# Local attention of a fused transformer kernel: from one head at a time to head pairs

## The chip, the cores and the metric

The kernel runs on one core of a Trainium2 chip. A core has five engines with an instruction stream each: TensorE (PE in the profile; its weight loads are listed as PEld), VectorE (DVE), ScalarE (ACT), GpSimd (POOL) and SyncE (SP), which issues the DMAs. They meet only through semaphores. The metric is the device time of one execution in microseconds (us); lower is better. The median of three runs is 1999.87 us.

## The reference, cut to what matters

The program is four layers of attention and feed-forward on a tensor `x` of 8 batches x 256 tokens x 128 channels. The change touches one function that runs twice: the windowed ("local") attention inside the third layer's feed-forward block.

```python
DIM, DEPTH, HEADS, DIM_HEAD, WINDOW = 128, 2, 8, 64, 64
qkv = shift_token(x) @ wqkv                       # q, k, v: 8 heads of 64
q, k = l2norm(q) * qs, l2norm(k) * ksc
q, k = rotary_xpos(q, k)                          # t*cos*scale + rotate_half(t)*sin*scale
# every window of 64 queries sees its own 64 keys and the 64 before them
sim = einsum('bhwid,bhwjd->bhwij', q * 8, k)
mask = (i < j) | (i > j + WINDOW) | (j == -1)
attn = softmax(where(mask, -max, sim))
o = einsum('bhwij,bhwjd->bhwid', attn, v)
x = x + o @ wo
```

Tokens 0 to 127 of a batch need keys 0 to 127. Tokens 128 to 255 need keys 64 to 255, since a query reaches at most 64 keys back.

## The kernel before, in words

`local_attention` is called for `layer` 0 and 1, with other stages between. It has a prologue, then eight batches (a loop of three rounds of two batches, then two batches written out), then a tail. Everything is float32; a float32 matmul is two passes in the trace, so "x2" is one matmul, except that the turns (transpositions) are one pass each.

**One head.** Per batch and head, TensorE computes scores for the two tiles of 128 queries (L2396: 128x128 for the first, L2397: 128x256 for the second). The queries `q` lie in 128 rows per head, 64 of them zero, so that a whole-array matmul against the keys of a head pair picks one head. VectorE adds the band mask, negates, and takes the minimum in one instruction per tile (`maxima`, L2188). ScalarE takes the exponentials and their row sums (`exponentials`, L2285). TensorE turns the 128x384 probabilities in three pieces (L2419) into a bank of PSUM, VectorE copies them out (L2204), and once both heads of a pair are copied, TensorE multiplies by V (L2388, L2391) in the two column halves of its array. These V products are called `GROUP`, `GROUP+1`, `GROUP+2`, and `LAST` for the fourth pair, which is done in the next batch.

**The ring.** All other results of TensorE go through a ring of four PSUM banks, `ring`. A `fill` on TensorE waits until the bank has been drained four fills earlier (`ring.free`), and a `drain` on ScalarE or VectorE waits until it is full. A batch has 18 fills: `QK`..`QK+3` (projections of q and k two batches ahead, L2345), `TURN`..`TURN+3` (turns of the normalised q and k of the next batch, four turns each, L2351), `V`, `V+1` (L2357), `LAST`, `SUMS` (turns the inverse sums, L2362), `SPREAD`, `SPREAD+1` (L2370), `OUT` (output projection, L2377) and the three `GROUP` fills. ScalarE drains all of these but `SPREAD` and `OUT`, which are VectorE's. The table `after` says behind which head each fill stands; `order` and `due` come from it.

**Order on each engine, per head n:** TensorE: scores of head n+2, turns of head n, then the fills due at n. ScalarE: exponentials of head n+2, then the drains due at n. VectorE: maxima of head n+2, the copy of head n, then drains, or a share of the preparation of later batches: `sum_squares`, `own_part` and `normalise`, each once for each 128-token tile j. `normalise(b, j)` ends with a multiply (L2149) that TensorE's `TURN` fills wait for. GpSimd computes the rotated halves (L2034), an inverse square root by `pow` (L2085) and the split of the inverse sums into three bfloat16 parts (L2064 to L2070).

**Prologue and tail.** Before the first scores, batches 0 and 1 are prepared (`AHEAD_OF_LOOP`, and on VectorE the loop `for b in range(2)`). After the last batch, `LAST`, `SUMS`, both `SPREAD` and `OUT` of the last batch are done one after another.

Of the kernel before, what the change touches and what calls it, by code (L numbers as in the profile page):

```python
# [1952 lines left out]
def local_attention(m, layer):  # L1953
# [24 lines left out]
    after = {QK: 1, QK + 1: 1, QK + 2: 2, QK + 3: 2, LAST: 1, SUMS: 2, TURN: 1, TURN + 1: 3, TURN + 2: 3, TURN + 3: 4, SPREAD: 5,  # L1978
             SPREAD + 1: 5, V: 4, V + 1: 6, OUT: 6}
    after.update({GROUP + g: 2 * g + 3 for g in range(NG - 1)})  # L1980

    SQUARED, SUMMED, OWN = (1, 4), (2, 6), (4, 6)
    order = sorted(range(PER), key=lambda f: (after[f], f < GROUP, f))
    due = [[f for f in order if after[f] == n] for n in range(NH)]
# [4 lines left out]
    with ExitStack() as ctx:  # L1989
# [47 lines left out]
        with nc.Block() as block:  # L2037
# [64 lines left out]
            def _(dve):  # L2102
# [859 lines left out]
```

## Time and profile before

| what | us |
|---|---|
| median of 3 runs | 1999.87 (1999.37 to 2002.19) |
| the profiled execution | 2002.39 |
| its span, first to last instruction | 2000.6 |
| local attention, layer 0: first to last batch's turns | 1147.80 to 1313.75 of the span |
| local attention, layer 1 | 1414.65 to 1582.77 of the span |

The two stages together take a sixth of the span. The page's busy shares over the whole program (PE 84%, DVE 65%, ACT 54%, POOL 27%) say little on them; the rows further down are from within the stages. In those rows a matmul's duration runs to its last result in PSUM, while the next one may start as soon as its columns have streamed. So what a matmul costs the engine is read from start to start.

### The profile page before, as it was taken

How to read it: one execution, taken by the hardware profiler on the slowest of the kernel's cores; microseconds unless marked ns; L12 is line 12 of the kernel's file. 1: busy time of each engine (PE TensorE's matmuls, PEld its weight loads, DVE VectorE, ACT ScalarE, POOL GpSimd, SP SyncE). 2: the span in 40 equal slices, each digit the busy share in tenths (PEclk: the TensorE clock that was granted, in tenths of full speed). 3: DMA queues.
4: the chain of work that ended last, by engine and by line, in shares of the span. 5: the costliest groups of instructions: out<-in, count | busy, mean ns of one | idle time of the engine just before them, and what ended most of it. 6: DMA issues, size and time to landing. Idle time of an engine off the chain costs nothing. (4 is left out here: it accounts for less than half of the span.)

```text
span 2000.6 us, 32933 instructions
## 1 busy us (share of the span) xinstructions
PE 1677.7 (84%) x10815; PEld 902.4 (45%) x10865; DVE 1305.7 (65%) x3417; ACT 1082.2 (54%) x2292; POOL 533.2 (27%) x609
## 2 busy tenths in 40 slices
PE   6769999963799999999997599976899786999933
PEld 4423333321455555555554366643566532333311
DVE  5447666645656666665666698854799546777746
ACT  3404666658455565555553477743777442666723
POOL 0326545110100000000000667413766133233000
PEclk9777999986899999999999799998999985999965
DMA  4224333010100000000000000000000022222000
GB/s 146 41 65 102 66 72 69 14 55 0 33 6 1 6 6 1 7 6 1 1 1 1 23 1 0 0 12 22 1 0 0 19 41 63 44 50 44 11 11 21
DMA packets 60188, 53.29 MB, mean 27 GB/s; under 512 B 9818, under 2 KB 52750, under 8 KB 59926
## 3 DMA queue, kind: packets, MB, share of 16 engines
q1 hardware_dynamic: 59190, 51.17, 11.1%
q8 instruction: 77, 1.26, 0.3%
q10 hardware_dynamic: 864, 0.39, 0.1%
q14 instruction: 57, 0.47, 0.1%
HBM read 30.44 MB, written 1.05 MB: 16 GB/s over the span
## 5 line engine op out<-in xcount | busy, mean ns | idle before, releaser
L1469 DVE CUSTOM_DVE_ANT_0 minus_s_l2x<-s_ps_l2x,mask_b_l2x 128x512 f32<-128x512 f32 x256 | 166.7, 689 | 193.9 <-PE s_ps_l2x L1639 193.8
L1552 ACT ACTIVATE probs_l2x<-minus_s_l2x,nmax_l2x 128x512 f32<-128x512 f32 x256 | 182.7, 715 | 184.2 <-DVE nmax_l2x L1469 184.2
L1026 DVE CUSTOM_DVE_ANT_0 junk_l1x<-s_ps_l1x,mask_b_l1x 128x512 f32<-128x512 f32 x256 | 166.4, 688 | 78.7 <-PE s_ps_l1x L1212 77.1
L1029 DVE TENSOR_REDUCE nmax_l3x<-s_ps_l3x 128x1 f32<-128x512 f32 x256 | 163.5, 685 | 56.1 <-PE s_ps_l3x L1212 54.4
L1078 ACT ACTIVATE pT_l1x<-st_ps_l1x 128x1024 f32<-128x1024 f32 x128 | 131.1, 1024 | 72.9 <-PE st_ps_l1x L1198 72.3
L1512 DVE COPY pT_l2x<-t_ps_l2x 128x512 f32<-128x512 f32 x256 | 164.3, 683 | 1.0 <-PE t_ps_l2x L1648 1.0
L2285 ACT ACTIVATE probs_l2a<-minus_s_l2a,nmax_l2a 128x128 f32<-128x128 f32 (+1 forms) x256 | 113.9, 447 | 89.1 <-DVE nmax_l2a L2188 87.1
L1648 PEld LDWEIGHTS t_ps_l2x<-consts,probs_l2x 128*128 128x128 f32 x1024 | 109.6, 141 | 96.9 <-issue 88.3
L1078 ACT ACTIVATE pT_l3x<-st_ps_l3x 128x1024 f32<-128x1024 f32 x128 | 130.1, 1022 | 35.3 <-PE st_ps_l3x L1198 33.8
L1648 PE MATMUL t_ps_l2x<-consts,probs_l2x 128*128 128x128 f32 x1024 | 139.8, 279 | 0.2 <-ACT probs_l2x L1552 0.2
L2034 POOL TENSOR_TENSOR other_l2a<-qk_l2a,tb_l2a 128x256 f32<-128x256 f32 x120 | 100.2, 866 | 44.9 <-ACT qk_l2a L2244 42.4
L2085 POOL TENSOR_TENSOR rn_l2a<-ssc_l2a,consts 128x16 f32<-128x16 f32 x32 | 95.1, 2977 | 51.6 <-DVE ssc_l2a L2125 51.3
L2188 DVE CUSTOM_DVE_ANT_0 minus_s_l2a<-s_ps_l2a,consts 128x128 f32<-128x128 f32 (+1 forms) x256 | 80.6, 352 | 33.1 <-PE s_ps_l2a L2397 30.6
L1224 PE MATMUL pv_ps_l3x<-pT_l3x,v_l3x 128*32 128x256 f32 x1024 | 82.5, 396 | 2.7 <-ACT o_l3x L1086 2.2
L1418 POOL TENSOR_TENSOR x_tok<-x_tok,bo_l2x 128x256 f32<-128x256 f32 x8 | 5.8, 724 | 289.4 <-DVE xn_l2x L1455 289.4
L1224 PE MATMUL pv_ps_l1x<-pT_l1x,v_l1x 128*32 128x256 f32 x1024 | 81.2, 391 | 1.0 <-ACT o_l1x L1086 0.9
L2397 PE MATMUL s_ps_l2a<-kT_l2a,q_l2a 128*128 128x256 f32 x256 | 78.7, 390 | 0.0
L1212 PE MATMUL s_ps_l3x<-kT_l3x_first,q_l3x 51*128 51x512 bf16 x192 | 65.0, 432 | 13.3 <-DVE nmax_l3x L1029 8.4
L1639 PE MATMUL s_ps_l2x<-kT_l2x_first,q_l2x 64*128 64x512 f32 x256 | 73.2, 649 | 1.9 <-ACT q_l2x L1534 1.5
L1639 PE MATMUL s_ps_l2x<-kT_l2x,q_l2x 64*128 64x512 f32 x256 | 72.3, 641 | 2.0 <-DVE nmax_l2x L1469 1.8
L1190 PE MATMUL st_ps_l1x<-maskT_b_l1x,consts_bf 128*128 128x512 bf16 x215 | 68.1, 383 | 4.7 <-issue 3.1
L2204 DVE COPY pT_l2a<-t_ps_l2a 128x384 f32<-128x384 f32 x128 | 70.7, 552 | 0.0
(480 smaller groups left out, 3654.3 us busy)
## 6 DMA issues: line engine op xcount, KB each, us to landing
kT_l1x_first<-parts_l1x_first SPq DMA_DIRECT2D x72, 64.0 KB
kT_l3x_first<-parts_l3x_first SPq DMA_DIRECT2D x72, 64.0 KB
mask_i_l1x<-in_mask SPq DMA_DIRECT2D x8, 512.0 KB, 3.8
maskT_i_l1x<-in_mask_t SPq DMA_DIRECT2D x8, 512.0 KB, 4.8
q_l1x<-parts_l1x_first SPq DMA_DIRECT2D x90, 32.0 KB
q_l3x<-parts_l3x_first SPq DMA_DIRECT2D x90, 32.0 KB
ctxT_l0x<-in_ctxT SPq DMA_DIRECT2D x9, 256.0 KB, 3.0
rows_l0x<-in_ctx SPq DMA_DIRECT2D x9, 256.0 KB, 4.0
```

The lines of the kernel that those rows point to most:

```text
L1026: dve.tensor_tensor_reduce(out=junk[w][:], in0=s_ps[w][:], in1=mask_b[b % 2][:, j, :], scale=-1.0, scalar=3e38, op0=ALU.add, op1=ALU.min, ...
L1029: dve.tensor_reduce(to, s_ps[w][:], AX.X, ALU.max, negate=True).then_inc(m.s_drained[w].sem, 1)
L1078: act.activation(pT[t % 4][:, :, 2 * j:2 * j + 2, :].rearrange("p w c t -> p w (c t)"), st_ps[j][:], ACT.Exp)\
L1224: ins = pe.matmul(pv_ps[32 * hh:32 * hh + 32, 0:S], v[b % NV][:, c, (4 * g + hh) * 32:(4 * g + hh + 1) * 32], pT[(2 * group + hh // 2) % 4 ...
L1469: dve.tensor_tensor_reduce(out=minus_s[n % 4][:], in0=s_ps[n % 2][:], in1=mask_b[b % 2][:], scale=-1.0, scalar=3e38, op0=ALU.add, op1=ALU. ...
L1512: dve.tensor_copy(pT[g % 2][:, hh, :, j * P:(j + 1) * P], t_ps[c % 2][:].rearrange("p (c t) -> p c t", t=P))\
L1552: act.activation(probs[n % 4][:], minus_s[n % 4][:], ACT.Exp, bias=nmax[:, b % 2, n:n + 1], scale=-1.0, accum_out=sums[:, b % 2, j, h:h + ...
L1639: pe.matmul(s_ps[n % 2][:], q[b % 2][rows, g, j * P:(j + 1) * P], kT[b % 2][rows, g, :], start=True, stop=True)\
L1648: ins = pe.transpose(t_ps[n % 2][:, c * P:(c + 1) * P], probs[n % 4][:, c * P:(c + 1) * P], k["ident"])
L2034: eng.tensor_tensor(other[:, j, w, :, to], qk[:, j, w, :, of], tb[:, w, j, to].unsqueeze(1).to_broadcast([P, NH, 32]), ALU.mult).then_inc( ...
L2085: pool.tensor_tensor(rn[:, cols], ssc[:, cols], k["minus_half"][:, 0:2 * NH], ALU.pow).then_inc(m.powers_ready.sem, 1)
L2285: act.activation(probs[n % (2 * DEEP)][:, cols], minus_s[n % (2 * DEEP)][:, cols], ACT.Exp, bias=nmax[:, u, TPB * n + j:TPB * n + j + 1], ...
```

## The change

1. **Scores of a pair.** `q` is stored like `k`, two heads in the 128 rows and no zeros. The two heads' scores are separate matmuls in the upper and lower 64 rows of the array, one PSUM bank each.
2. **192 keys.** The second tile's scores, mask, exponentials cover keys 64 to 255 rather than 0 to 255. The columns of `probs` that are no longer written are zeroed once by GpSimd.
3. **Steps of a pair.** The loop goes over four steps rather than eight heads. TensorE: scores of pair s+1, the V product of the pair before (first fill of the step), turns of both heads of pair s, the other fills of `due[s]`. ScalarE: copy of the second head's turned probabilities, exponentials of pair s+1, drains. VectorE: maxima of pair s+1, copy of the first head's turned probabilities, its other work.
4. **Fill order.** `due` is written out: (`LAST`, `QK`, `QK+1`, `QK+2`), (`GROUP`, `TURN`..`TURN+3`, `SUMS`), (`GROUP+1`, `SPREAD`, `SPREAD+1`, `QK+3`, `V`), (`GROUP+2`, `V+1`, `OUT`). `SUMS` stands last in step 1.
5. **Preparation.** `normalise(b+2, 0)` is done in step 2 of batch b and `normalise(b+1, 1)` in step 0; before, both were of batch b+1, behind heads 0 and 1. The prologue therefore normalises tile 0 of batch 1 too, ahead of the first maxima. The reciprocal of the sums stands at the head of step 0, and GpSimd takes the `pow` of tile 0 before it rotates tile 1.
6. **ScalarE** drains q with one 128-row instruction in place of two of 64 rows.

```diff
-    TILES = (slice(0, P), slice(P, BAND))
+    TILES = (slice(0, P), slice(P + 64, BAND))
...
+    STEPS = NH // 2
+    due = [[LAST, QK, QK + 1, QK + 2],
+           [GROUP, TURN, TURN + 1, TURN + 2, TURN + 3, SUMS],
+           [GROUP + 1, SPREAD, SPREAD + 1, QK + 3, V],
+           [GROUP + 2, V + 1, OUT]]
...
                     for j in range(TPB):
                         sum_squares(b, j)
                         own_part(b, j, at)
-                    if b == 0:
-                        for j in range(TPB):
+                        if b == 0:
                             other_half(dve, j, 1)
+                        if (b, j) != (1, 1):
                             normalise(b, j)
...
+                        if s == 0 and left >= 1:
+                            normalise(b + 1, 1)
+                        if s == 2:
+                            for f in range(SPREAD, OUT):
+                                drain(i, u, f, turn(i, u, f))
+                            if left >= 2:
+                                normalise(b + 2, 0)
+                        if s == 3:
+                            if left >= 2:
+                                sum_squares(b + 2, 1)
+                                own_part(b + 2, 1, at)
+                            drain(i, u, OUT, turn(i, u, OUT))
...
+                    for s in range(STEPS):
+                        act.wait_ge(*ring.full(*group_before(i, u, s)))
+                        act.wait_ge(*m.turned.after(NH * b + 2 * s + 2))
+                        act.activation(pT[s % 2][:, 1].rearrange("p c t -> p (c t)"), t_ps[1][:, 0:BAND], ACT.Copy).then_inc(m.unit_copied[1].sem, 1)
+                        if s + 1 < STEPS or left >= 1:
+                            exponentials(*ahead(i, u, s + 1))
+                        for f in due[s]:
+                            drain(i, u, f, turn(i, u, f), unused=f < (LAST, TURN, 0)[left])
...
+                    halves = [(s_ps[hh], slice(HD * hh, HD * (hh + 1))) for hh in range(2)]
+                    for out, rows in halves:
+                        pe.matmul(out[:, 0:P], q[u][rows, g, 0:P], kT[u][rows, g, 0:P], start=True, stop=True)
+                    for out, rows in halves:
+                        pe.matmul(out[:, TILES[1]], q[u][rows, g, P:S], kT[u][rows, g, 64:S], start=True, stop=True).then_inc(m.scores_ready.sem, 1)
...
+                        if s + 1 < STEPS or left >= 1:
+                            pe.wait_ge(*m.max_ready.after(TPB * (NH * b + 2 * s + 2)))
+                            scores(*ahead(i, u, s + 1))
+                        fill(i, u, due[s][0], turn(i, u, due[s][0]), unused=due[s][0] < (LAST, TURN, 0)[left])
+                        pe.wait_ge(*m.probs_ready.after(TPB * (NH * b + 2 * s + 2)))
+                        for n in (2 * s, 2 * s + 1):
+                            pe.wait_ge(*m.unit_copied[n % 2].after(STEPS * b + s))
+                            for c in range(3):
+                                ins = pe.transpose(t_ps[n % 2][:, c * P:(c + 1) * P], probs[n % (2 * DEEP)][:, c * P:(c + 1) * P], k["ident"])
+                            ins.then_inc(m.turned.sem, 1)
+                        for f in due[s][1:]:
+                            fill(i, u, f, turn(i, u, f), unused=f < (LAST, TURN, 0)[left])
```

How the instructions stand; rows that only prepare registers or repeat the row above them are left out. First TensorE, before, from the second turns of batch 0 (`ring0` to `ring3` are the ring's banks, `t_ps` the banks of turned probabilities; `bankN_drained` is the ring's wait):

```order
L2419 MATMUL t_ps1_l2a0<-consts,probs1_l2a0 128x128 [waits turned_copied]
L2345 MATMUL ring0_l2a0<-wqkv_l2a0,hs0_l2a0 128x512 [waits bank0_drained]
L2345 MATMUL ring1_l2a0<-wqkv_l2a0,hs0_l2a0 128x512 [waits bank1_drained]
L2351 MATMUL ring2_l2a0<-consts,own_l2a0 128x128 [waits bank2_drained]
L2388 MATMUL ring3_l2a0<-pT1_l2a0,v1_l2a0 64x256 [waits bank3_drained]
L2396 MATMUL s_ps0_l2a0<-kT0_l2a0,q0_l2a0 128x128 [waits max_ready]
L2397 MATMUL s_ps0_l2a0<-kT0_l2a0,q0_l2a0 128x256
L2419 MATMUL t_ps0_l2a0<-consts,probs2_l2a0 128x128 [waits turned_copied]
```

And TensorE in the changed kernel, step 1 of batch 0, from its V product (`GROUP`, bank 0) to `SUMS` (bank 1):

```order
L2390 MATMUL ring0_l2a0<-pT0_l2a0,v0_l2a0 64x256 [waits bank0_drained]
L2424 MATMUL t_ps0_l2a0<-consts,probs2_l2a0 128x128 [waits even_unit_copied,probs_ready]
L2424 MATMUL t_ps1_l2a0<-consts,probs3_l2a0 128x128 [waits odd_unit_copied]
L2352 MATMUL ring1_l2a0<-consts,own_l2a0 128x128 [waits bank1_drained,normed]
L2352 MATMUL ring2_l2a0<-consts,own_l2a0 128x128 [waits bank2_drained]
L2352 MATMUL ring3_l2a0<-consts,own_l2a0 128x128 [waits bank3_drained,normed]
L2352 MATMUL ring0_l2a0<-consts,own_l2a0 128x128 [waits bank0_drained]
L2363 MATMUL ring1_l2a0<-consts_bf,inv_parts_l2a0 48x128 [waits bank1_drained,inv_split]
```

The V product has moved ahead of the turns, both heads' turns stand together, and five ring fills follow them in a row; the fourth of these takes bank 0, which the V product of the same step has filled.

ScalarE, before, around the same place:

```order
L2285 ACTIVATE probs3_l2a0,sums_l2a0<-minus_s3_l2a0,nmax_l2a0 128x256 [waits max_ready]
L2244 ACTIVATE qk_l2a0<-ring0_l2a0 128x512 [waits bank0_filled]
L2244 ACTIVATE qk_l2a0<-ring1_l2a0 128x512 [waits bank1_filled]
L2251 ACTIVATE q1_l2a0<-ring2_l2a0 64x4x128 [waits bank2_filled]
L2252 ACTIVATE q1_l2a0<-ring2_l2a0 64x4x128
L2267 ACTIVATE o1_l2a0<-ring3_l2a0 128x256 [waits bank3_filled]
```

ScalarE in the changed kernel, step 1 of batch 0:

```order
L2295 ACTIVATE pT1_l2a0<-t_ps1_l2a0 128x384 [waits turned]
L2285 ACTIVATE probs0_l2a0,sums_l2a0<-minus_s0_l2a0,nmax_l2a0 128x128 [waits max_ready]
L2285 ACTIVATE probs0_l2a0,sums_l2a0<-minus_s0_l2a0,nmax_l2a0 128x192 [waits max_ready]
L2285 ACTIVATE probs1_l2a0,sums_l2a0<-minus_s1_l2a0,nmax_l2a0 128x128 [waits max_ready]
L2285 ACTIVATE probs1_l2a0,sums_l2a0<-minus_s1_l2a0,nmax_l2a0 128x192 [waits max_ready]
L2266 ACTIVATE o0_l2a0<-ring0_l2a0 128x256 [waits bank0_filled]
L2250 ACTIVATE q1_l2a0<-ring1_l2a0 128x4x128 [waits bank1_filled]
L2255 ACTIVATE kT1_l2a0<-ring2_l2a0 128x4x128 [waits bank2_filled]
L2250 ACTIVATE q1_l2a0<-ring3_l2a0 128x4x128 [waits bank3_filled]
L2255 ACTIVATE kT1_l2a0<-ring0_l2a0 128x4x128 [waits bank0_filled]
L2262 ACTIVATE invT_l2a0<-ring1_l2a0 48x256 [waits bank1_filled]
```

Before, ScalarE waits for VectorE's maxima and for full banks only. Now each step begins with a copy that waits for the turns of both heads of the pair, and the exponentials and all drains of the step stand behind it.

VectorE in the prologue of the changed kernel, batch 1, up to the first maxima; the two rows on `own` between the first own part and the second sum of squares are the added ones:

```order
L2119 TENSOR_REDUCE ss_l2a<-sq_l2a 128x16
L2123 TENSOR_SCALAR ssc_l2a<-ss_l2a 128x16
L2131 TENSOR_TENSOR own_l2a<-qk_l2a,ta_l2a 128x1024
L2142 TENSOR_TENSOR own_l2a<-own_l2a,other_l2a 128x1024
L2146 TENSOR_TENSOR own_l2a<-own_l2a,rn_l2a 128x1024
L2119 TENSOR_REDUCE ss_l2a<-sq_l2a 128x16
L2123 TENSOR_SCALAR ssc_l2a<-ss_l2a 128x16
L2131 TENSOR_TENSOR own_l2a<-qk_l2a,ta_l2a 128x1024
L2186 ISA minus_s_l2a,nmax_l2a<-s_ps_l2a,consts 128x128
```

A `normalise` (add and multiply) has moved from the first batch to a place ahead of the first maxima.

## Rows read from the trace of the kernel before

**Rows 1.** Busy time in stretches: the layers' batches, and a short stretch of slow clock.

```profile
core 0: us, PE busy (x) PEld busy (x) DVE busy (x) ACT busy (x) POOL busy (x), PEclk, DMA share, GB/s
1147.80:1281.80 134.00, 128.94 (x830) 90.61 (x828) 121.06 (x323) 102.62 (x311) 91.58 (x85) 1.00 0.00 0
1281.80:1302.40 20.60, 18.05 (x132) 13.81 (x130) 15.07 (x49) 13.85 (x48) 2.69 (x4) 1.00 0.00 1
1414.65:1549.20 134.55, 129.83 (x830) 91.20 (x828) 120.45 (x323) 102.79 (x310) 91.17 (x84) 0.99 0.00 1
1549.20:1571.40 22.20, 19.65 (x132) 14.89 (x130) 15.27 (x49) 14.30 (x49) 2.69 (x4) 0.92 0.01 1
1553.40:1557.00 3.60, 3.60 (x13) 2.69 (x14) 2.88 (x7) 2.42 (x8) 0.00 (x0) 0.53 0.00 0
```

**Rows 2.** Timeline of TensorE in one batch: start, us, instruction, idle before.

```profile
1194.90 0.65 PE L2351 MATMUL ring_l2a<-consts,own_l2a 128*128 128x128 f32 x4 [1.00 <-DVE own_l2a L2149]
...
1208.77 1.95 PE L2377 MATMUL ring_l2a<-wo_l2a,o_l2a 128*128 128x128 f32 x16
1210.55 0.39 PE L2396 MATMUL s_ps_l2a<-kT_l2a,q_l2a 128*128 128x128 f32 x2
...
1211.21 0.49 PE L2419 MATMUL t_ps_l2a<-consts,probs_l2a 128*128 128x128 f32 x3
1211.63 0.65 PE L2388 MATMUL ring_l2a<-pT_l2a,v_l2a 128*64 128x256 f32 x4
...
1212.43 0.49 PE L2396 MATMUL s_ps_l2a<-kT_l2a,q_l2a 128*128 128x128 f32 x2
...
1213.19 0.49 PE L2419 MATMUL t_ps_l2a<-consts,probs_l2a 128*128 128x128 f32 x3
```

**Rows 3.** Timeline of TensorE in the wide attention, whose scores use the halves.

```profile
1007.49 1.02 PE L1606 MATMUL ring_l2x<-wv_l2x_first,ctxT_l2x 128*128 128x512 f32 x2
1008.44 1.13 PE L1639 MATMUL s_ps_l2x<-kT_l2x_first,q_l2x 64*128 64x512 f32 x4
1009.50 0.77 PE L1648 MATMUL t_ps_l2x<-consts,probs_l2x 128*128 128x128 f32 x5
```

**Rows 4.** Timeline of ScalarE in one batch.

```profile
1201.38 0.40 ACT L2285 ACTIVATE probs_l2a<-minus_s_l2a,nmax_l2a 128x128 f32<-128x128 f32 x1
...
1201.77 0.50 ACT L2285 ACTIVATE probs_l2a<-minus_s_l2a,nmax_l2a 128x256 f32<-128x256 f32 x1
...
1202.26 0.37 ACT L2267 ACTIVATE o_l2a<-ring_l2a 128x256 f32<-128x256 f32 x1
1202.53 0.59 ACT L2256 ACTIVATE kT_l2a<-ring_l2a 128x512 f32<-128x512 f32 x1
1203.00 0.59 ACT L2251 ACTIVATE q_l2a<-ring_l2a 64x512 f32<-64x512 f32 x1
```

**Rows 5.** Timeline of TensorE, ScalarE and VectorE at the end of layer 0.

```profile
1313.42 0.49 PE L2419 MATMUL t_ps_l2a<-consts,probs_l2a 128*128 128x128 f32 x3
...
1315.91 0.29 PE L2362 MATMUL ring_l2a<-consts_bf,inv_parts_l2a 128*48 128x128 bf16 x2 [0.28 <-POOL inv_parts_l2a L2070]
1316.67 0.61 PE L2370 MATMUL ring_l2a<-invT_l2a,consts_bf 128*128 128x256 bf16 x4 [0.47 <-ACT invT_l2a L2263]
...
1316.24 0.38 ACT L2263 ACTIVATE invT_l2a<-ring_l2a 48x256 bf16<-48x256 f32 x1 [0.18 <-PE ring_l2a L2362]
...
1313.96 0.55 DVE L2204 COPY pT_l2a<-t_ps_l2a 128x384 f32<-128x384 f32 x1
1314.43 0.24 DVE L2172 RECIPROCAL inv_l2a<-sums_l2a 128x16 f32<-128x16 f32 x1
```

**Rows 6.** Timeline of VectorE and TensorE at the first batch of layer 0.

```profile
1143.64 0.28 DVE L2188 CUSTOM_DVE_ANT_0 minus_s_l2a<-s_ps_l2a,consts 128x128 f32<-128x128 f32 x1
...
1147.35 1.16 DVE L2145 TENSOR_TENSOR own_l2a<-own_l2a,other_l2a 128x1024 f32<-128x1024 f32 x1
...
1149.79 0.28 DVE L2188 CUSTOM_DVE_ANT_0 minus_s_l2a<-s_ps_l2a,consts 128x128 f32<-128x128 f32 x1
...
1147.46 0.49 PE L2419 MATMUL t_ps_l2a<-consts,probs_l2a 128*128 128x128 f32 x3
```

More of the change, by code:

```diff
@@ L1976, in local_attention @@
     PER = GROUP + NG - 1
[L1978 to L1984, printed above, removed]
+    STEPS = NH // 2
[3 more added lines that the diff above has]
+           [GROUP + 2, V + 1, OUT]]
+    order = sum(due, [])
     SHIFTS, TURNS = 2, NT // 4
@@ L2248, in drain @@
                         act.wait_ge(*ring.full(*at))
-                        bank = ring.bank(*at[1:])[:].rearrange("p (g t) -> p g t", t=P)
-                        act.activation(q[1 - u][0:HD, 0:NH:2, cols], bank[0:HD], ACT.Copy)
-                        act.activation(q[1 - u][HD:P, 1:NH:2, cols], bank[HD:P], ACT.Copy).then_inc(ring.drains(*at[1:]), 1)
+                        act.activation(q[1 - u][:, :, cols], ring.bank(*at[1:])[:].rearrange("p (g t) -> p g t", t=P), ACT.Copy)\
+                            .then_inc(ring.drains(*at[1:]), 1)
                     if TURN <= f < V and (f - TURN) % 2:
@@ L2289, in _, with exponentials @@
-                for n in range(DEEP):
-                    exponentials(0, 0, n)
+                def exponentials(i, u, g):
+                    for n in (2 * g, 2 * g + 1):
+                        for j, cols in enumerate(TILES):
+                            act.wait_ge(*m.max_ready.after(TPB * (NH * (2 * i + u) + n) + j + 1))
+                            act.activation(probs[n % (2 * DEEP)][:, cols], minus_s[n % (2 * DEEP)][:, cols], ACT.Exp,
+                                           bias=nmax[:, u, TPB * n + j:TPB * n + j + 1], scale=-1.0,
+                                           accum_out=sums[:, u, j, n:n + 1]).then_inc(m.probs_ready.sem, 1)
@@ L2291, in attend @@
+                exponentials(0, 0, 0)
                 def attend(i, u, left=2):
                     b = 2 * i + u
-                    for n in range(DEEP, NH + DEEP):
-                        if n < NH or left >= 1:
-                            exponentials(*ahead(i, u, n))
-                        for f in due[n - DEEP]:
-                            drain(i, u, f, turn(i, u, f), unused=f < (LAST, TURN, 0)[left])
-                        if n - DEEP in SQUARED and left >= 2:
-                            square(b + 2, SQUARED.index(n - DEEP), lambda f: turn(i, u, f))
@@ L2300, in attend @@
-                    if left == 0:
-                        return
-                    act.wait_ge(*ring.full(*turn(i, u, V + TPB - 1)))
-                    act.sem_inc(m.passed.sem, 1)
-                    act.activation(hs[1 - u][:], hT[:, bass.ds((b + 3) * S, S)], ACT.Copy).then_inc(m.h_moved.sem, 1)
+                    for s in range(STEPS):
+                        act.wait_ge(*ring.full(*group_before(i, u, s)))
[4 more added lines that the diff above has]
+                        for f in due[s]:
+                            if f in (QK, QK + 2) and left >= 2:
+                                act.wait_ge(*m.rotated.after(4 * TPB * (b + 1) + 4 * (f // 2 + 1)))
+                            drain(i, u, f, turn(i, u, f), unused=f < (LAST, TURN, 0)[left])
+                            if f in (QK + 1, QK + 3) and left >= 2:
+                                square(b + 2, (f - QK) // 2, lambda f: turn(i, u, f))
+                            if f == V + 1 and left >= 1:
+                                act.activation(hs[1 - u][:], hT[:, bass.ds((b + 3) * S, S)], ACT.Copy).then_inc(m.h_moved.sem, 1)
@@ L2403, in _ @@
                     pe.wait_ge(*ring.empty(*prepared(0, f)))
-                for n in range(DEEP):
-                    scores(0, 0, n)
+                scores(0, 0, 0)
                 pe.wait_ge(*m.ready_made.after(8))
```

101 lines of the change are left out of this document (36 added, 65 removed).

## Prediction

> **What bounds the kernel now.** The page gives PE 84% over the whole program, which says nothing on two short stages, so I went from the stages' windows [rows 1] to the timelines of TensorE [rows 2, 3], ScalarE [rows 4] and the two ends of a stage [rows 5, 6]. The profiled execution took 2002.39 us, its span 2000.6; the median of three is 1999.87. The sum is made against the profiled one, and its difference is carried to the median.
>
> In layer 0 the first six batches take 134.0 us, 22.3 each, with PE busy 128.9 (96%), DVE 121.1 (90%), ACT 102.6 (77%) [rows 1]. So TensorE sets the pace, and VectorE is close behind. The one wait that shows on TensorE is for the normalised tile, 1.0 us idle [rows 2]; counted by start times it is 1.2. With 0.15 of small gaps a batch is some 21.1 of matmul time and 1.3 of waits. The question is whether the change shortens TensorE's work and leaves it as free of waits.
>
> **TensorE's work.** From start to start [rows 2]: scores of one head 0.66 (1210.55 to 1211.21), and 0.76 straight after a V product (1212.43 to 1213.19); three turns ahead of a V product 0.42 (1211.21 to 1211.63), of which 0.33 is their stream (a record of 0.49 less a tail of 0.16 to PSUM), so 0.11 a turn and 0.09 for the change into halves; the V product with its way out 0.80 (1211.63 to 1212.43); `OUT` 1.78 (1208.77 to 1210.55). A four-turn fill is 4 x 0.11 = 0.44, `SUMS` two such passes, 0.22, both `SPREAD` four, 0.45 (record 0.61) [rows 5]. A 512-wide fill is 0.95 less the 0.09 of the change that follows it = 0.86 [rows 3].
>
> Scores of a pair in the halves aren't in this function's trace, but the wide attention has them: two heads, 512 columns, four records, 1.06 us [rows 3]. One 512-wide float32 matmul is 0.86, so the two heads run side by side, and 0.20 is way in and out. For 128 + 192 = 320 columns: 0.86 x 320/512 = 0.54, + 0.20, + 0.09 for the change from the whole array = 0.84 a pair (I take this). Before, a pair was 0.66 + 0.76 = 1.42. Bounds: 0.54 if all overheads hide; 2 x 0.54 + 0.2 = 1.27 if passes this short do not overlap. V product 0.80 and six turns 0.66 + 0.06 for the way back follow. So each step has 0.84 + 0.80 + 0.71 = 2.35 before its other fills, four steps 9.4. The other fills: step 0 three projections 2.58; step 1 four turned 1.74 and `SUMS` 0.22; step 2 `SPREAD` 0.45, `QK+3` and `V` 1.72; step 3 `V+1` 0.86 and `OUT` 1.78. Sum 9.35. TensorE's work is 18.75 a batch, 2.35 less than 21.1. The wait of 1.2 goes too: both tiles are normalised a step or more ahead of their turns. If that were all, a batch would lose about 3.5 us, until VectorE holds it up.
>
> The Trainium skill, TensorEngine Tiling (Array Packing), Key Properties under Tiling Modes, says that a change of tiling mode drains the engine. The trace agrees with 0.09 in and 0.10 out around a V product; with the rule the pair's scores are 0.84, without it 0.64.
>
> **The new wait.** In the changed kernel every step of ScalarE starts with a copy that waits for the turns of both heads, and the pair's exponentials and all the step's drains come after it. Count from the moment T at which the step's last turn has left TensorE. Turn to reader: a 0.27 record after a 0.11 stream leaves 0.17 of tail, then 0.04 (record end 1316.20, ScalarE 1316.24) [rows 5], so the copy starts at 0.21. A copy of 256 takes 0.27 and one of 512 0.47 [rows 4], so one of 384 0.37: 0.58. The exponentials of a head took 0.88 from 1201.38 to 1202.26; the shorter second one saves 64 x (0.50 - 0.40)/128 = 0.05: 0.83 a head, 1.67 a pair: 2.25. The drain of the step's V product (record 0.37) ends at 2.62, and TensorE sees it 0.05 to 0.1 later (1316.62 to 1316.67) [rows 5]: 2.70.
>
> The ring has four banks, so the fourth fill behind a V product needs that drain. In step 1 it is `TURN+3`, which TensorE reaches at 3 x 0.44 = 1.31: wait 1.4. In step 2 it is `V`, reached at 0.45 + 0.86 = 1.31: wait 1.4. `SUMS` waits some 0.05 for the first q drain. At the batch's end TensorE waits until `V+1` is drained, at 2.25 + 0.27 + 0.59 + 0.08 = 3.2, and gets there at 2.64: 0.55. In step 0 the fourth fill is `GROUP` of step 1, at 2.58 + 0.84: no wait. Step lengths: step 0 4.93, step 1 2.70 + 0.44 + 0.28 + 2.35 = 5.77, step 2 2.70 + 0.86 + 2.35 = 5.91, step 3 3.2 + 2.35 = 5.54. Sum 22.15 against 22.3 to 22.45. Behind each of these waits stand the next scores, thus VectorE's maxima, thus ScalarE's next exponentials: the whole cycle waits with it.
>
> The other engines: VectorE loses four copies (0.47 each (1313.96 to 1314.43) [rows 5]) and some 8 x 0.07 of maxima, 20.2 to 17.8 busy; its longest step, 2, has a normalise of 2.44 (1147.35 to 1149.79) [rows 6], a copy, two heads' maxima (by the share of the columns 1.0) and both `SPREAD` drains (an estimate: a third wider than a copy, 1.3), 5.2, inside 5.9. ScalarE: + 4 x 0.37, - 8 x 0.05, - 2 x 0.7 (one 128-row q copy for two 0.6 ones), 17.1 to 16.8. GpSimd's 15.3 a batch [rows 1] is unchanged, and its new order brings each `pow` in front of the normalise that needs it. All hidden by the steps above. So the 3.5 us are given back as 3.4 of ring waits, nearly all.
>
> **Start and end of a stage.** In the prologue VectorE now normalises tile 0 of batch 1 before the first maxima: + 2.44, and the multiply waits for GpSimd's `pow`, which starts only behind the sum of squares just done: + 0.3, an estimate. The sum of squares of batch 0's tile 1 also moves behind a normalise, so its `pow` and TensorE's turns come later, of which ScalarE's shorter q copies give a part back: + 0.5, an estimate. First maxima 3.2 later than 1143.64. Then two heads' maxima and exponentials, scores, V product and six turns must be done before step 0 ends: 1151.5 against 1147.79 for the two first heads now (1147.46 + 0.33) [rows 6]. Start: + 3.7.
>
> Batch 6 has no projections, so its step 0 is bound by the exponentials (2.42 + 0.71 = 3.13): 3.13 + 5.77 + 5.91 + 5.54 = 20.35 against 20.6 [rows 1]. Batch 7, whose skipped fills still wait for their bank: 3.13 + 5.3 + 4.3 = 12.75 against 11.4 (1302.38 to 1313.75). Tail: `OUT` of batch 6 now stands behind the last turns (1.78) and VectorE drains it before the last reciprocal, which comes 2.4 after the last turns instead of 0.7 (1313.75 to 1314.43) [rows 5]: + 1.7.
>
> **Sum.** Layer 0: six batches 132.9 against 134.0, - 1.1; batch 6 - 0.25; batch 7 + 1.4; start + 3.7; tail + 1.7: + 5.4. Layer 1: 132.9 against 134.55, - 1.65; batch 6 20.35 against 22.2, - 1.85 (1.6 of it a slow-clock stretch that layer 0 doesn't have); + 1.4; start + 3.4 (its prologue's first batch is 0.3 slower already); tail + 1.7: + 3.0. Together + 8.4: 2010.8 for the profiled execution, 2008.3 for the median. What a measurement can't tell from no change is 0.2%, 4 us: 1995.9 to 2003.9. With the period off by 0.35 on 12 batches and the two ends by 1.5, this case's own range is 2001 to 2016.
>
> **Rivals.**
>
> *The ring does not hold TensorE back* (the copy or drains are faster, or the bank order differs from my reading). Then a batch is TensorE's 18.75 or VectorE's 17.8 plus what the two cost each other, 1.2 today: some 19.7. 12 x (22.15 - 19.7) = 29 less: 1979. For it: all four engines have less work or the same. Against it: the order rows show the waits on bank 0. The Trainium skill, TensorEngine Tiling, PSUM Bottleneck under Performance Considerations, advises ScalarE and VectorE both for evacuation, as the change does; by that rule it would come out so, since VectorE sheds 1.9 us a batch. No run here shows it yet.
>
> *The scores are cheaper than 0.84*, down to 0.54: 4 x 0.2 x 12 to 4 x 0.3 x 12 = 10 to 14 less: 1994 to 1999. For it: 0.20 of way in and out was read from one place. Against: V products show the same gaps.
>
> *The short passes don't overlap*: 1.27 a pair, + 0.43 x 4 x 12 = 21: 2029. Against it: V product's 128-wide passes overlap (two heads' 384 columns, two passes each, in 0.64).
>
> *The clock falls.* After 2.6 us without a matmul TensorE was granted half speed for 3.6 us in layer 1 (0.53 [rows 1]), the lower of its two levels, and batch 6 took 1.6 more than in layer 0; waits of 1.4 could do the same. This ends slower: decided by TensorE's idle stretches of 1.4 us, twice a batch; one fall in every second batch is 6 x 1.6 = 10 more: 2018. Against it: the 1.0 us wait of every batch today never did.
>
> **Chances.** Ring waits as worked out 0.47 (faster 0.04, same 0.07, slower 0.36); cheaper scores 0.20 (0.03, 0.15, 0.02); ring doesn't hold 0.13 (all faster); clock 0.12 and no overlap 0.08 (all slower). Faster 0.20, same 0.22, slower 0.58. The range 1990 to 2026 leaves out the ring case and the far half of the no-overlap case.
>
> **What would show it.** Right: idle of 1.2 to 1.6 before the fourth `TURN` fill and before the `V` fill, released by ScalarE's drain of `o`; no wait of a `TURN` fill for the normalising multiply; pair scores 0.8 to 0.9 from start to start; batches of 22 us; first maxima 3 us later; last reciprocal 2.4 behind the last turn. Wrong: PE busy with no gap in step 1, batches near 20, or half-speed stretches inside the loop.

## The result, and the profile after

The changed kernel takes 2037.58 us (median of 4 runs, 2035.25 to 2040.69) against 1999.96 of the kernel before: ratio 1.018, 95% interval 1.0165 to 1.0196. It is slower by 1.8%, clear of the noise and in the direction that was forecast, but by 37.6 us and not by 8.4, which lies outside the range of 1990 to 2026. The profiled execution took 2038.94, its span 2037.1.

Busy time in stretches, the answer to [rows 1]: the loop's six batches, batch 6 and batch 7 of layer 0, and the six of layer 1.

```profile
core 0: us, PE busy (x) PEld busy (x) DVE busy (x) ACT busy (x) POOL busy (x), PEclk, DMA share, GB/s
1156.06:1290.61 134.55, 116.31 (x830) 76.10 (x828) 108.09 (x301) 102.31 (x324) 100.12 (x80) 1.00 0.00 0
1290.61:1313.64 23.03, 17.50 (x132) 12.61 (x130) 10.66 (x43) 13.16 (x48) 3.66 (x9) 0.93 0.00 1
1313.64:1330.62 16.98, 10.32 (x67) 7.11 (x65) 5.10 (x22) 7.56 (x31) 0.00 (x0) 0.70 0.00 0
1446.46:1580.85 134.39, 116.15 (x830) 76.07 (x828) 108.28 (x301) 102.31 (x324) 97.75 (x81) 1.00 0.00 1
```

TensorE's busy time in the loop fell from 128.94 to 116.31, 2.1 a batch, and VectorE's from 121.06 to 108.09; yet the six batches take 134.55 against 134.0. A batch is counted from the last turn of its first step to the same place in the next batch; batch 7, the last, ends at the last turn of its fourth step. Batch 7 took 11.37 before and 16.98 now, at a granted clock of 0.70.

What TensorE waited for in layer 0 (in total, times, longest):

```profile
PE s_ps_l2a L2400 <- DVE nmax_l2a L2186: 10.5, 1, 10.5
PE ring_l2a L2358 <- ACT o_l2a L2266: 9.2, 7, 2.1
PE ring_l2a L2352 <- ACT o_l2a L2266: 8.4, 7, 1.3
PE ring_l2a L2390 <- ACT o_l2a L2266: 3.8, 2, 1.9
PE s_ps_l2a L2400 <- ACT v_l2a L2259: 3.8, 6, 0.9
PE ring_l2a L2363 <- ACTq L2240: 2.8, 1, 2.8
PE ring_l2a L2390 <- ACTq L2240: 1.9, 1, 1.9
```

The second, third and fifth are the three waits of the prediction: for the fill `V`, for `TURN+3`, and at the batch's end, where TensorE stood idle for 0.43 and, where the loop closes, for 0.93 (0.55 was predicted). In the loop the first two took 1.19 and 1.18 to 1.27 each; the 2.1 is that of batch 6. The other rows were not in the prediction. Timelines of TensorE and ScalarE in step 1 (last turn at 1161.43), answering to [rows 2, 4]:

```profile
1164.08 0.66 PE L2352 MATMUL ring_l2a<-consts,own_l2a 128*128 128x128 f32 x4 [1.18 <-ACT o_l2a L2266]
...
1164.89 0.49 PE L2400 MATMUL s_ps_l2a<-kT_l2a,q_l2a 64*128 64x128 f32 x4
1165.22 0.49 PE L2402 MATMUL s_ps_l2a<-kT_l2a,q_l2a 64*128 64x192 f32 x4
1165.64 0.65 PE L2390 MATMUL ring_l2a<-pT_l2a,v_l2a 128*64 128x256 f32 x4
...
1166.45 0.87 PE L2424 MATMUL t_ps_l2a<-consts,probs_l2a 128*128 128x128 f32 x6
```

```profile
1161.63 0.49 ACT L2295 ACTIVATE pT_l2a<-t_ps_l2a 128x384 f32<-128x384 f32 x1 [0.22 <-PE t_ps_l2a L2424]
1162.02 0.39 ACT L2285 ACTIVATE probs_l2a<-minus_s_l2a,nmax_l2a 128x128 f32<-128x128 f32 x1
...
1163.66 0.37 ACT L2266 ACTIVATE o_l2a<-ring_l2a 128x256 f32<-128x256 f32 x1
```

T is again the moment at which the step's last turn has left TensorE. ScalarE: copy at T + 0.20, exponentials, then the V product's drain from T + 2.23; `TURN+3` starts at T + 2.65 (predicted 2.70). A pair's scores took 0.75 from start to start (0.84 was worked out from [rows 3]).

The start of the stage, VectorE and TensorE, against [rows 6]:

```profile
1143.45 1.22 DVE L2142 TENSOR_TENSOR own_l2a<-own_l2a,other_l2a 128x1024 f32<-128x1024 f32 x1
1146.28 1.66 DVE L2146 TENSOR_TENSOR own_l2a<-own_l2a,rn_l2a 128x1024 f32<-128x1024 f32 x1 [1.60 <-POOL rn_l2a L2083]
...
1150.88 0.28 DVE L2186 CUSTOM_DVE_ANT_0 minus_s_l2a<-s_ps_l2a,consts 128x128 f32<-128x128 f32 x1
```

```profile
1140.69 0.49 PE L2400 MATMUL s_ps_l2a<-kT_l2a,q_l2a 64*128 64x128 f32 x4
...
1151.99 0.80 PE L2400 MATMUL s_ps_l2a<-kT_l2a,q_l2a 64*128 64x128 f32 x4 [10.48 <-DVE nmax_l2a L2186]
```

The first scores lie ready from 1141.5 on; VectorE takes them at 1150.88 (1143.64 before), and TensorE, idle for 10.48, comes back at half speed (a group of 0.49 takes 0.80).

Batch 6, step 0, and the tail, against [rows 5]:

```profile
1293.41 1.12 PE L2390 MATMUL ring_l2a<-pT_l2a,v_l2a 128*64 128x256 f32 x4 [1.89 <-ACT o_l2a L2266]
...
1330.62 1.95 PE L2378 MATMUL ring_l2a<-wo_l2a,o_l2a 128*128 128x128 f32 x16
...
1337.13 3.21 PE L2378 MATMUL ring_l2a<-wo_l2a,o_l2a 128*128 128x128 f32 x16 [1.32 <-DVE o_l2a L2158]
```

No projections stand in step 0 of batches 6 and 7, so `GROUP` reaches `LAST`'s bank at once and waits until ScalarE is through its exponentials. In batch 6 this is the step that grew: from step 0 to step 3 they took 5.51, 5.99, 6.03 and 5.50 (predicted 3.13, 5.77, 5.91 and 5.54). In batch 7, where the turns are skipped too, `SUMS` in step 1 waits in the same way:

```profile
1321.62 0.38 PE L2363 MATMUL ring_l2a<-consts_bf,inv_parts_l2a 128*48 128x128 bf16 x2 [2.84 <-ACTq L2240]
```

Its steps 0 to 2 took 4.83, 7.53 and 4.61 (predicted 3.13, 5.3 and 4.3). The granted clock was 0.66 from 1316.4 to 1319, behind a wait of 1.89, and 0.50, the lower of TensorE's two levels, from there to 1327.

### The profile page after: what moved, and what is told of

It is laid out like the page before. It is cut to its first block and busy times, and to the rows that moved or that the text cites. A ratio compares the mean times of both kernels' runs of the same rounds, so it can differ in the third digit from the quotient of the medians.

```text
span 2037.1 us, 32961 instructions
## 1 busy us (share of the span) xinstructions
PE 1649.7 (81%) x10815; PEld 868.9 (43%) x10865; DVE 1270.3 (62%) x3353; ACT 1078.5 (53%) x2324; POOL 549.8 (27%) x613
## 5 line engine op out<-in xcount | busy, mean ns | idle before, releaser
L2083 POOL TENSOR_TENSOR rn_l2a<-ssc_l2a,consts 128x16 f32<-128x16 f32 x32 | 124.0, 3876 | 51.5 <-DVE ssc_l2a L2123 51.5
L2285 ACT ACTIVATE probs_l2a<-minus_s_l2a,nmax_l2a 128x128 f32<-128x128 f32 (+1 forms) x256 | 105.6, 417 | 15.2 <-DVE nmax_l2a L2186 15.2
L2186 DVE CUSTOM_DVE_ANT_0 minus_s_l2a<-s_ps_l2a,consts 128x128 f32<-128x128 f32 (+1 forms) x256 | 67.7, 320 | 72.6 <-PE s_ps_l2a L2402 72.6
L2295 ACT ACTIVATE pT_l2a<-t_ps_l2a 128x384 f32<-128x384 f32 x64 | 31.5, 492 | 103.5 <-PE t_ps_l2a L2424 103.5
L1212 PE MATMUL s_ps_l3x<-kT_l3x_first,q_l3x 51*128 51x512 bf16 x192 | 64.2, 427 | 13.8 <-DVE nmax_l3x L1029 8.1
L2352 PE MATMUL ring_l2a<-consts,own_l2a 128*128 128x128 f32 x256 | 38.0, 297 | 45.0 <-DVE own_l2a L2146 28.0
```

Of the source, the lines that this page charges most:

```text
L2083: pool.tensor_tensor(rn[:, cols], ssc[:, cols], k["minus_half"][:, 0:2 * NH], ALU.pow).then_inc(m.powers_ready.sem, 1)
L2285: act.activation(probs[n % (2 * DEEP)][:, cols], minus_s[n % (2 * DEEP)][:, cols], ACT.Exp, bias=nmax[:, u, TPB * n + j:TPB * n + j + 1], ...
```

## The experiments

The table gives each kernel's median and its ratio to the kernel before on the same chip. The other columns are read from the traces, in us: "stage" is the two layers' sum from VectorE's copy that opens the stage (`hb_l2a`) to the one that opens the next (`hb_l2f`), then, of layer 0, the first maxima and T(0), the last turn of step 0 (before: of the second head), counted from that copy, two batches of the loop in a row, batch 6, batch 7, and the tail from the last turn. Outside the stage, where all kernels are alike, profiled runs differ by up to 6 us at either end of the program, so a step is judged by its own column.

| kernel | us | ratio (95%) | stage | maxima | T(0) | batches | 6 | 7 | tail |
|---|---|---|---|---|---|---|---|---|---|
| before | 1999.96 | 1 | 435.3 | 39.1 | 43.3 | 22.4, 22.5 | 20.6 | 11.4 | 7.7 |
| after | 2037.58 | 1.018 (1.0165-1.0196) | 472.0 | 47.2 | 52.4 | 22.1, 22.7 | 23.0 | 17.0 | 10.5 |
| e1_early_v | 1990.11 | 0.9945 (0.9925-0.9964) | 420.6 | 47.1 | 52.3 | 20.1, 20.6 | 17.5 | 9.5 | 11.1 |
| e2_gpsimd_order | 2037.38 | 1.0169 (1.0144-1.0194) | 469.4 | 46.2 | 51.4 | 22.1, 22.7 | 22.6 | 16.6 | 10.1 |
| e3_old_prep | 2040.15 | 1.0192 (1.0164-1.022) | 470.2 | 38.2 | 43.4 | 22.6, 24.6 | 23.0 | 17.0 | 10.5 |
| e4_before_halves | 1992.67 | 0.9948 (0.9931-0.9965) | 423.6 | 38.1 | 41.8 | 21.9, 22.0 | 21.0 | 10.5 | 7.7 |
| e5_before_192 | 1986.92 | 0.9935 (0.9909-0.9961) | 423.2 | 38.4 | 42.5 | 21.7, 21.7 | 19.8 | 11.0 | 9.0 |
| e6_no_end_wait | 1980.62 | 0.9902 (0.9879-0.9925) | 412.3 | 46.4 | 51.6 | 19.9, 19.9 | 17.3 | 9.5 | 9.3 |
| e7_split_exp | 1974.15 | 0.9869 (0.9846-0.9892) | 406.4 | 47.2 | 52.4 | 19.4, 19.3 | 16.9 | 9.5 | 9.3 |
| e8_max_first | 1975.57 | 0.9879 (0.9853-0.9905) | 408.3 | 39.7 | 43.0 | 20.1, 20.6 | 17.5 | 9.5 | 9.3 |
| e9_early_v_last_two | 2016.28 | 1.0079 (1.0055-1.0103) | 446.9 | 47.2 | 52.4 | 22.1, 22.7 | 17.5 | 9.5 | 10.9 |
| c1_all | 1959.89 | 0.9794 (0.9768-0.9819) | 392.6 | 38.6 | 43.5 | 19.4, 19.3 | 16.8 | 9.5 | 9.3 |
| c2_out_ahead | 1959.95 | 0.9796 (0.9772-0.9819) | 397.3 | 37.8 | 43.0 | 19.6, 19.4 | 17.5 | 11.0 | 9.4 |
| e10_own_first | 1978.4 | one run | 412.4 | 47.2 | 52.4 | 19.9, 19.3 | 17.5 | 9.5 | 10.9 |

**e1_early_v.** ScalarE drains the V product ahead of its copy:

```diff
+  drain(i, u, due[s][0], turn(i, u, due[s][0]), unused=...)
   act.wait_ge(*ring.full(*group_before(i, u, s)))
   ...
-  for f in due[s]:
+  for f in due[s][1:]:
```

> The changed kernel with one move: ScalarE drains the V product (the step's first fill) ahead of the copy for which it waits, not behind the pair's exponentials. Theory (the ring's banks, held by ScalarE's late drain of the V product, set steps 1 and 2 and step 0 of the last two batches): step 2 shrinks from 5.97 to about 5.2 (VectorE's work there), step 3 by 0.3, step 1 by only 0.2, since SUMS then waits for the drain of TURN, which still stands behind the exponentials; step 0 of batches 6 and 7 loses its wait of 1.9. Batches of 21.0 instead of 22.4, stage ends 2 to 4 us a layer earlier besides: 2010 to 2018 us. Rival (the loop is held by VectorE, by the loop's own branch, or by the clock): 2030 or more, and the wait moves to another instruction with the steps unchanged.

Steps 1 to 3 became 5.42, 4.51 and 5.23 or 5.72 (expected 5.55, 5.2 and 5.2). 47 us went, where 20 to 27 were expected: batch 6 lost 5.5 and batch 7 lost 7.5, and the loop's batches lost 2.1 and not 1.4. The same windows as above, and the waits of layer 0:

```profile
1152.03:1273.93 121.90, 113.46 (x828) 76.51 (x827) 108.20 (x297) 103.63 (x324) 94.72 (x80) 1.00 0.00 1
1273.93:1291.45 17.52, 15.56 (x133) 11.37 (x131) 10.75 (x46) 13.40 (x49) 4.54 (x9) 1.00 0.00 1
1291.45:1300.92 9.47, 7.26 (x67) 5.01 (x65) 5.16 (x23) 7.54 (x32) 0.00 (x0) 1.00 0.00 1
```

```profile
PE ring_l2a L2364 <- ACT q_l2a L2250: 7.4, 7, 1.1
PE s_ps_l2a L2401 <- ACT v_l2a L2259: 2.2, 6, 0.7
```

The waits on `o` are gone, the one of `SUMS` on the first q drain is new, as expected, and the clock of batches 6 and 7 is back at 1.00 from 0.93 and 0.70. In the changed kernel it was 1.00 up to 1292.5 and 0.62 from there to 1296, around the end of the wait of 1.89.

**e9_early_v_last_two.** The same edit under `if left < 2` only.

> The changed kernel with the early V drain in the last two batches alone; the six of the loop as changed. Theory (what made batches 6 and 7 long is the same late drain, which no projection covers there): 5.5 less in batch 6 and 7.5 in batch 7 of each layer, 2008 to 2014 us, the six before at 22.4 as they were. Rival (their length comes from the skipped fills or from the slow clock): 2025 or more.

Batches 6 and 7 as in e1, the loop as in the changed kernel; 21 us less, 2 us short of the expected range, since the stage gave 25 but the rest of the program 4 back. So the late drain cost about as much in the last two batches of each layer (25 us of stage) as in the twelve of the loops (26).

**e2_gpsimd_order.** GpSimd rotates tile 1 of batch 0 ahead of its first `pow`.

> The changed kernel, with GpSimd rotating both tiles of batch 0 before its first pow in the prologue, as before; nothing else. Theory (normalise of tile 0 waits for rotated halves of tile 1, which stand behind a pow of 3.8 us): that wait of 3.5 us goes, first maxima some 3 us earlier in each layer, 2031 to 2033 us. Rival (the multiply that waits for pow ends last anyway, or TensorE's projections do): under 1 us a layer, 2036 to 2038.

The time is the rival's: 2037.38, and the first maxima gained 1.0. The wait of 3.54 went, and the turns of tile 1 came 2.1 earlier. But TensorE ran at half speed for longer (passes of 1.06 where they take 0.59 at full speed), so that `V+1` and the fill behind it took 1.71 and 1.14 from start to start instead of 0.91 and 0.85.

**e3_old_prep.** `normalise` of both tiles in step 0, and the prologue as before:

```diff
    if s == 0 and left >= 1:
+       normalise(b + 1, 0)
        normalise(b + 1, 1)
    ...
-           if left >= 2:
-               normalise(b + 2, 0)
```

> The changed kernel with part 5 undone: both tiles of a batch normalised one batch ahead, here both in step 0; no normalise of batch 1 ahead of the loop; batch 0 and GpSimd in the old order. Theory (the start of a stage is late by the preparation, and the loop is held by the ring): first maxima back at some 1143.5, last turns of step 0 at 1148.6 instead of 1156.1, steady batches unchanged at 22.4 since the ring's wait in step 1 ends later than that for the normalised tile: 2020 to 2026 us. Rival 1 (the start is late because a pair must be done and the clock is low): 2033 or more. Rival 2 (VectorE's 6.6 us in step 0 is late for the turns): batches over 23, 2035 or more.

Half right. The start is the preparation's: T(0) is back at 43.4, so neither the pair nor the clock makes it late. But rival 2 holds as well: step 1 grew from 5.72 or 5.78 to 7.92, 7.57 and 7.79 in batches 1, 3 and 4 and to 6.20 and 6.35 in 2 and 5. The two starts gained 16.9 us and the stage as a whole 1.8: the loops lost most of it.

**e4_before_halves, e5_before_192.** The kernel before with pair scores in the halves, 192 keys and one q drain; and with 192 keys alone (`TILES`, `kT[..., 64:S]`, zeroed columns of `probs`):

```diff
-  if n + DEEP < NH or left >= 1:
-      pe.wait_ge(*m.max_ready.after(TPB * (NH * b + n + 1)))
+  if n % 2 == 0 and (n + DEEP < NH or left >= 1):
+      pe.wait_ge(*m.max_ready.after(TPB * (NH * b + n + 2)))
```

> The kernel before with parts 1, 2 and 6 alone: pair scores in the array's halves, issued ahead of the turns of the even head, 192 keys, q drained at once; order, eight heads and the ring's table as before. Theory (the scores are 0.84 instead of 1.42 a pair, and it is the new order that gave it back): TensorE's work falls by 2.35 a batch and VectorE, 19.6 busy, becomes nearly the bound: batches of about 20.8, 1970 to 1980 us. Rival 1 (passes this short do not overlap in the halves): batches of 22 or more, 1990 to 2000. Rival 2 (waits take the place at once, since the pair's scores need both maxima): 1995 to 2010.

> The kernel before with 192 keys for the second tile alone. TensorE's work falls by 0.86 a batch, VectorE's by 0.6, ScalarE's by 0.4. Theory (from the run with both parts, whose batches took 22.0 though TensorE's work fell by 2.35: VectorE holds the old order): nearly the same gain as with both, 1992 to 1995 us. Rival (TensorE paces the old order, and the halves themselves gain nothing): 1985 to 1988.

e5 went by the rival: 192 keys alone give 13.5 us, 0.7 a batch of the 0.86 that TensorE saves. TensorE still paces that kernel: over three batches (1165 to 1230) it is busy for 62.62 of 65.00, and its one wait is 0.8 a batch. e4 ended at 1992.67, within the range of its first rival, but the mechanism is that of its second: passes this short do overlap, since a pair's scores cost 0.75 there too, and yet the halves on top give nothing (batches 21.9 against 21.7), because waits take their place. TensorE in e4:

```profile
1209.43 0.49 PE L2395 MATMUL s_ps_l2a<-kT_l2a,q_l2a 64*128 64x128 f32 x4 [1.14 <-DVE nmax_l2a L2188]
...
1214.12 0.65 PE L2349 MATMUL ring_l2a<-consts,own_l2a 128*128 128x128 f32 x4 [1.34 <-DVE own_l2a L2149]
```

A pair's scores wait for both heads' maxima, and the turns for `normalise`: 2.5 a batch between them, both on VectorE. In the old order the halves don't pay.

**e6_no_end_wait.** On top of e1:

```diff
-  for f in range(V, LAST):
-      pe.wait_ge(*ring.empty(*turn(i, u, f)))
```

> The changed kernel with the early V drain, and without TensorE's wait for the drains of V and V+1 at a batch's end (the fourth fill after V+1, QK+1, waits for that bank in any case). Theory: TensorE stands idle 0.66 there, and in the round that closes the loop its sequencer adds 0.5 for the branch, since nothing is queued behind a wait; without the wait the branch is hidden. Step 3 of 5.23 and 5.73 becomes 4.6 to 4.8 in both, batches 19.5 (VectorE's work is 18.2): 1976 to 1982 us, and odd and even batches alike. Rival (the extra 0.5 is VectorE's or ScalarE's loop, or VectorE takes over): 1986 to 1990, and every second batch stays 0.5 longer.

The time is the theory's. Step 3 came out longer than its 4.6 to 4.8: it takes 5.00 in every batch, and the difference between odd and even is gone. In the changed kernel TensorE's sequencer came out of that wait at 1198.42 and reached the scores at 1199.04, a branch record of 0.22 between them; in the even batch, without the branch, it took 0.12 from its last record to the scores.

**e7_split_exp.** On top of e6, in step 1 the drain of `TURN` between the two heads' exponentials:

```diff
+  first = () if s + 1 >= STEPS and left < 1 else (0,) if s == 1 else (0, 1)
+  ...
+      if n == 1 and first == (0,):
+          exponentials(*ahead(i, u, s + 1), (1,))
```

> As the run without the end wait, and in step 1 ScalarE drains TURN between the exponentials of the pair's two heads. Theory: SUMS waits 1.05 for that bank in every batch, step 1 of 5.42 becomes 4.6; TensorE alone would give 18.7 a batch, VectorE 18.2 plus its waits: 19.0, 0.5 to 1.0 less a batch than without: 1966 to 1974 us. Rival (VectorE is the bound by then, or the second head's exponentials come too late for the turns): within 3 us of the run without the end wait.

The mechanism is the theory's, the gain smaller: step 1 from 5.42 to 4.9 (4.6 was expected), 6.5 us less, and 1974.15 is just above the range.

**e8_max_first.** On top of e1, in VectorE's prologue:

```diff
   own_part(b, j, at)
+  if (b, j) == (1, 0):
+      maxima(0, 0, 0)
```

> The changed kernel with the early V drain, and in the prologue VectorE takes the first pair's maxima behind own_part of batch 1's tile 0, ahead of normalise(1, 0) and of the work on tile 1. Theory (the first scores lie ready for 9 us behind VectorE's preparation): first maxima 7 us earlier, but the second pair's maxima stay behind the normalise, so that the stage gains 4 to 6 us a layer: 1978 to 1983 us. Rival (what is moved only shifts the wait to the second pair, since the same VectorE work has to be done before it): 1987 to 1991.

Maxima 7.5 and T(0) 9.3 earlier; the first batch gives 3.6 back (20.5 to 24.1), as the second pair's maxima still stand behind the normalise. Net 12.3 of stage in the two layers, a little more than the 8 to 12 expected. The tails have little part in it: layer 0's is 1.7 shorter, layer 1's 1.0 longer. The median fell by 14.5, below the expected range.

**c1_all.** e7, e8 and e2 together.

> All moves that gained, together: early V drain, no end wait, exponentials split in step 1, first maxima ahead of normalise(1, 0), GpSimd rotating both tiles of batch 0 first. Theory (they act at different places): 1974 less 10 to 13 for the two starts and 2 for GpSimd: 1959 to 1965 us. Rival (VectorE, now the busiest beside TensorE, can't make up the work that the early maxima push back): 1968 or more.

As expected, and 2.1% under the kernel before. In two batches of the loop TensorE is busy 98% (37.78 of 38.70 us):

```profile
1170.00:1208.70 38.70, 37.78 (x279) 25.59 (x278) 36.18 (x98) 34.40 (x108) 33.47 (x29) 1.00 0.00 1
```

**c2_out_ahead.** On top of c1:

```diff
-  [GROUP + 2, V + 1, OUT]]
+  [GROUP + 2, OUT, V + 1]]     # the first two ahead of the turns
```

> As all moves together, and OUT of a batch stands ahead of the last step's turns instead of behind V+1. Theory (OUT behind the last turns is what lengthened the tail, and step 2 is VectorE's longest while TensorE has less there): tail 10.5 becomes 7.5 to 8.5 in each layer, batches equal or 0.3 shorter: 3 to 7 us under all moves together. Rival (turns and thus exponentials of the next step come 1.8 later, and nothing covers it): batches 0.5 longer, 3 to 6 us over.

Refuted: no gain (1959.95 against 1959.89), and the stage of the profiled run is 4.7 longer. The last reciprocal came 0.75 after the last turn instead of 2.33, but then the last `OUT` ran at half speed, and the 1.6 was gone; batches 6 and 7 grew by 0.6 and 1.5. The first row is c1's, the second c2's:

```profile
1299.67 2.02 PE L2386 MATMUL ring_l2a<-wo_l2a,o_l2a 128*128 128x128 f32 x16 [1.32 <-DVE o_l2a L2161]
```

```profile
1295.45 3.65 PE L2386 MATMUL ring_l2a<-wo_l2a,o_l2a 128*128 128x128 f32 x16 [1.32 <-DVE o_l2a L2161]
```

**e10_own_first.** On top of e7, in the loop `own_part` ahead of `sum_squares`.

> As the run with split exponentials; in the loop VectorE does own_part ahead of the sum of squares, not behind it. Theory on GpSimd's pow (3.81 to 3.93 us in the changed kernel, 2.90 before, because it starts while VectorE's own_part runs and waits for its end): pow back at 2.9 in the loop, still 3.8 in the prologue. Rival (it is the new order on GpSimd itself, pow between rotations): 3.8 to 3.9 everywhere. The time stays within 4 us of the run with split exponentials, since nothing in the loop waits for pow.

All 24 `pow` of the two loops took 2.90 to 2.92, the 8 of the prologues 3.81 to 3.88: the theory holds. The time, of one run, is 4.3 above e7's, a little over the 4 expected, and the stage is 6.0 longer. Step 1 of every second batch takes 5.4 to 5.5 instead of 4.95 and the tails 1.6 more. Why was not looked into; `own_part` now stands beside the rotations and takes 1.68 to 1.82 in more than half of its places. GpSimd's `pow` and VectorE in e7, then in e10:

```profile
1190.84 3.81 POOL L2083 TENSOR_TENSOR rn_l2a<-ssc_l2a,consts 128x16 f32<-128x16 f32 x1 [1.58 <-DVE ssc_l2a L2123]
...
1190.67 1.22 DVE L2131 TENSOR_TENSOR own_l2a<-qk_l2a,ta_l2a 128x1024 f32<-128x1024 f32 x1
```

```profile
1182.55 2.91 POOL L2083 TENSOR_TENSOR rn_l2a<-ssc_l2a,consts 128x16 f32<-128x16 f32 x1 [0.83 <-DVE ssc_l2a L2123]
```

## Why the prediction was wrong

Its terms against the traces, in us of both layers together:

| term | predicted | measured |
|---|---|---|
| loops, 12 batches | -2.75 | +0.35 |
| batch 6 | -2.1 | +3.3 |
| batch 7 | +2.8 | +11.2 |
| start | +7.1 | +17.6 |
| tail | +3.4 | +4.2 |
| all else | 0 | -0.2 |
| sum (of spans) | +8.4 | +36.5 |

*TensorE's work and the ring waits of the loop: right.* Both ring waits stood where they were foreseen, 1.2 long each in the loop for 1.4, and steps 0 to 2 took 4.93, 5.72 to 5.79 and 5.97 for 4.93, 5.77 and 5.91. The gain on TensorE, 2.1 a batch, was given back to the waits. e1 shows it by taking the drain forward. The rivals of an unheld ring and of passes that do not overlap are out. The scores cost 0.75, cheaper than 0.84 by 0.09, but not by the 0.2 to 0.3 of that rival.

*The end-of-batch wait was undersized.* Its 0.55 was worked out as idle time of the array; where the loop closes it costs 0.5 more, shown by e6. This is some 2 of the 3.1 that the loops were off; 0.7 more is step 0 of each layer's batch 0 (5.37 and 5.24 for 4.93; the granted clock was 0.84 over its first 2.4 us in layer 0), and 0.7 step 2 with 5.97 for 5.91.

*Batches 6 and 7: the step that failed most, 13.8.* "In step 0 the fourth fill is `GROUP` of step 1, at 2.58 + 0.84: no wait" was worked out with three projections in the step, and then used for the two batches that have none, as "its step 0 is bound by the exponentials"; the 5.3 and 4.3 of batch 7 were given without a working. There the fourth fill comes at once and waits 1.9: step 0 of batch 6 took 5.51 for 3.13, which is nearly all that this batch was off. In batch 7 the chain through the exponentials closes in every step, and `SUMS` waits 2.8. The rival on the clock had its mechanism, idle TensorE, but the wrong place: it fell around these waits and not around those of 1.4 in the loop, where the granted clock was 1.00. e1 and e9 undo the waits and the slow clock together, so what each cost by itself is not shown.

*The start: 10.5.* The term counted `normalise` (2.44), 0.3 for `pow` and 0.5 for the turns. Measured from the stage's opening, the first scores started 3.8 later (36.98 for 33.17 in layer 0) and the maxima 4.2 later still. The 3.8 comes from the chain of batch 0: tile 1's sum of squares and its `pow` start only when tile 0 is normalised, and that normalise waits, by its count, for tile 1's rotated halves too. The term had 0.5 for this chain; e2 shows that the count is 1.0 of it. In the 4.2, next to the `normalise`, the `pow` of batch 1 took 3.81 (2.89 before), so that the multiply waited 1.60 and not 0.3. Another 1.0 lies between the maxima and T(0) (5.18 for 4.15), where TensorE's granted clock was 0.50; 0.5 was foreseen. e3 shows that the preparation is all of the late start, e8 that most of it can be had back.

*Tail: right in kind* (reciprocal 2.33 behind the last turn, 2.4 foreseen), with 1.1 more in layer 0 than foreseen, where the last `OUT` ran at a slow clock (3.21, against 1.95 of the `OUT` before it). Behind "all else" stands 3.6 more in the stage between the layers, which opened at a granted clock of 0.71 (0.92 before), against 3.8 less before and behind the stages, for which no experiment was made.

*What lay behind the ring.* With the ring freed (c1) the new order runs at 19.3 a batch. The rival "the ring does not hold" gave 19.7.

## What to carry to other kernels

An engine that both computes the next critical input and empties a small ring should empty it first: a drain of 0.37 behind 1.67 of exponentials cost 47 us here, and moving one line gave them back. Work out a ring's waits once for each different batch, the peeled last ones too, since fills that are left out bring the fourth fill forward. And a wait at the end of the loop's body cost more here than its idle time, since the branch then stood in the open (0.93 idle against 0.43); the ring's own wait made it needless.

## What the runs showed of the hardware

**VectorE and GpSimd.** A `pow` of 128x16 on GpSimd that starts while VectorE's `own_part`, with two inputs from SBUF, is running took 3.80 to 3.93, and one that starts without it 2.89 to 3.17, in all 14 traces; the difference of 0.9 is about what was left of `own_part` (1.22 long, begun 0.17 earlier). The other way round, in e10, `own_part` took 1.68 to 1.82 in place of 1.22 where a rotation had gone first, and a rotation that came behind it took 1.71 to 1.74 in place of 0.73. The Trainium skill, SBUF — State Buffer, SBUF: two separate sides, says that the two engines' shared pair of ports goes to the one that starts first for its whole instruction. The rows of `pow` and of `own_part` agree with it.

**The branch of a loop.** It cost 0.5 on TensorE where its sequencer came out of a wait with nothing queued (5.72 against 5.23 for step 3 in e1), and nothing in e6, where work was queued (5.00 in every batch).

**A gain ahead of a stretch at half clock can be taken back.** In e2 turns that came 2.1 earlier were followed by more passes at half clock, and the scores came only 1.0 earlier. In c2 the last reciprocal came 1.6 earlier, the last `OUT` took 3.65 instead of 2.02, and the tail was no shorter (9.4 against 9.3).
